# A two-stage feed-forward and attention kernel: the value product from split squares, one block later

## The reference

```python
x = x + 0.5 * ffn(layernorm(x), W_r, W_k, W_v, mu_r, mu_k)
x = x + attn(layernorm(x), Wk, bk, Wv, bv, ln_g, ln_b, Wo, bo)   # attn adds its own input too
x = x + 0.5 * ffn(layernorm(x), W_r, W_k, W_v, mu_r, mu_k)

# ffn: x_prev is x shifted by one token
xr = mu_r * x + (1.0 - mu_r) * x_prev
xk = mu_k * x + (1.0 - mu_k) * x_prev
out = sigmoid(xr @ W_r) * (square(relu(xk @ W_k)) @ W_v)
```

## Time and profile before

| engine | busy | share of the span |
|---|---|---|
| TensorE (PE) | 656.5 | 87% |
| TensorE weight loads (PEld) | 542.1 | 72% |
| VectorE (DVE) | 611.3 | 81% |
| ScalarE (ACT) | 418.0 | 56% |
| GpSimd (POOL) | 569.6 | 76% |

### The profile page before, as it was taken

How to read it: one execution, slowest core, us unless ns; L and a number is a source line. 1 busy time by engine, 2 the same in 40 slices (tenths; PEclk the granted TensorE clock), 3 DMA queues, 4 the chain that set the end, 5 groups by cost and what they waited for, 6 DMA issues and landing times. The chain is left out here.

```text
span 751.9 us, 13029 instructions
## 1 busy us (share of the span) xinstructions
PE 656.5 (87%) x3536; PEld 542.1 (72%) x3536; DVE 611.3 (81%) x1378; ACT 418.0 (56%) x743; POOL 569.6 (76%) x879
## 2 busy tenths in 40 slices
PE   2888988999779989988988998898867988988897
PEld 2777878888656667766766676676646878878786
DVE  5868667755679999999999999999976668667744
ACT  4666666664534544554455455445446676666652
POOL 3777778776378888888888888888853877788764
PEclk9999999999988999999999999999979999999999
DMA  7710000000000000000000000000000011011102
GB/s 246 231 57 0 0 0 0 0 1 1 0 0 1 1 0 0 0 0 0 0 0 0 0 0 0 0 0 1 1 1 0 29 57 56 30 54 56 56 29 85
DMA packets 18442, 18.67 MB, mean 25 GB/s; under 512 B 752, under 2 KB 18160, under 8 KB 18416
## 3 DMA queue, kind: packets, MB, share of 16 engines
q1 hardware_dynamic: 18416, 18.36, 7.5%
HBM read 9.97 MB, written 8.39 MB: 24 GB/s over the span
## 5 line engine op out<-in xcount | busy, mean ns | idle before, releaser
L222 POOL TENSOR_TENSOR bhalf<-xn 128x128 f32<-128x128 f32 x256 | 118.3, 493 | 30.4 <-DVE xn L567 30.4
L1135 PE MATMUL bank<-wkv,m_xnT 128*128 128x256 f32 x512 | 135.5, 395 | 5.3 <-DVE khat L561 3.3
L409 DVE TENSOR_TENSOR gating_buffers<-bank,gating_buffers 128x1024 f32<-128x1024 f32 x31 | 38.0, 1225 | 95.8 <-issue 55.0
L1079 PE MATMUL bank<-wffn,kact 128*128 128x256 f32 x512 | 115.8, 379 | 0.0
L1135 PEld LDWEIGHTS bank<-wkv,m_xnT 128*128 128x128 f32 x512 | 92.5, 196 | 25.1 <-issue 4.6
L953 POOL TENSOR_TENSOR res<-res,gating_buffers 128x1024 f32 (+1 forms) x31 | 75.2, 2426 | 39.1 <-DVE gating_buffers L409 39.1
L1079 PEld LDWEIGHTS bank<-wffn,kact 128*128 128x128 f32 x512 | 94.8, 190 | 11.6
L284 POOL TENSOR_TENSOR xk_lo<-xk,xk_hi 128x1024 fp32r<-128x1024 f32 x30 | 71.2, 2372 | 33.4 <-ACT xk_hi L712 33.4
L946 POOL TENSOR_TENSOR xr_lo<-xr,xr_hi 128x1024 fp32r<-128x1024 f32 x32 | 76.0, 2374 | 19.0 <-ACT xr_hi L718 16.8
L567 DVE TENSOR_TENSOR xn<-bank,khat 128x1024 f32<-128x1024 f32 x64 | 77.8, 1216 | 1.4
L567 DVE TENSOR_TENSOR gating_buffers<-bank,khat 128x1024 f32<-128x1024 f32 x64 | 77.6, 1212 | 0.0
(11 more groups left out here) (108 smaller groups left out, 1691.7 us busy)
## 6 DMA issues: line engine op xcount, KB each, us to landing
res<-x SPq DMA_DIRECT2D x16, 512.0 KB, 4.5
out<-res SPq DMA_DIRECT2D x15, 512.0 KB, 2.9
wkv<-w_kv SPq DMA_DIRECT2D x1, 512.0 KB, 8.0
out<-res SPq DMA_DIRECT2D x2, 256.0 KB, 2.1
wffn<-w_k SPq DMA_DIRECT2D x1, 256.0 KB, 3.8
wffn<-w_r SPq DMA_DIRECT2D x1, 256.0 KB, 4.6
wffn<-w_v SPq DMA_DIRECT2D x1, 256.0 KB, 6.0
wo<-w_o SPq DMA_DIRECT2D x1, 256.0 KB, 7.2
```

The costliest lines, as they stand in the source:

```text
L222: last = engine.tensor_tensor(o, a, b, op)
L1079: last = nc.tensor.matmul(dst[:, i, :], x[:, f, i * P:(i + 1) * P], wffn[:, w, f, :], start=f == 0, stop=f == FC - 1)
L1135: nc.tensor.matmul(dst[:, i, :], m_xnT[:, f, i * P:(i + 1) * P], wkv[:, f, col:col + D], start=f == 0, stop=False)
```

## The change

The square of the key product is written back to PSUM, over `k_ps`. It is then split as `xk` and `xr` are: ScalarE rounds it to `kact_hi` (`square_high`), VectorE subtracts this into `kact_lo` (`square_low`), both in fp32r and with two buffers, one for each b. The value product runs in three fp32r passes from these, for block s-1 behind key product s on TensorE. The weights of the value product are split too. On VectorE the receptance mixes come ahead of the squares, and gating of block s-1 behind them, followed by the low parts. GpSimd's program is unchanged. `bound` of the middle stage, which lay in `kact`, has its own buffer. Cut to its core:

```diff
-        wffn_hi = sb("wffn_hi", [P, 2, FC, D], F32R)
-        wffn_lo = sb("wffn_lo", [P, 2, FC, D], F32R)
+        wffn_hi = sb("wffn_hi", [P, 3, FC, D], F32R)
+        wffn_lo = sb("wffn_lo", [P, 3, FC, D], F32R)
...
-        kact = sb("kact", [P, FC, CW])
+        kact_hi = sb("kact_hi", [P, 2, FC, CW], F32R)
+        kact_lo = sb("kact_lo", [P, 2, FC, CW], F32R)
...
-        bound = kact[:, :, :].rearrange("p b (t n) -> p b t n", n=D)
+        bound = sb("bound", [P, 2, 2, D])
...
                     dve.wait_ge(e["relu_done"], 2 * s + o + 1)
-                    need(dve, e["v_done"], 2 * s)
-                    nc.vector.tensor_tensor(kact[:, o, :], relu_k[:, o, :], k_ps[:, o, :], ALU.mult).then_inc(e["kact_done"], 1)
+                    nc.vector.tensor_tensor(k_ps[:, o, :], relu_k[:, o, :], k_ps[:, o, :], ALU.mult).then_inc(e["kact_done"], 1)
+
+                def square_low(j, b, o):
+                    s = 2 * j + b
+                    dve.wait_ge(e["kacthi_done"], 2 * s + o + 1)
+                    need(dve, e["v_done"], 2 * (s - 1))
+                    nc.vector.tensor_tensor(kact_lo[:, b, o, :], k_ps[:, o, :], kact_hi[:, b, o, :].bitcast(F32),
+                                            ALU.subtract).then_inc(e["kactlo_done"], 1)
...
-                        if has(b, -1):
-                            gating(*at(j, b, -1))
                         if mixing:
                             difference(nj, nb)
                             mix_key(nj, nb, 0)
                             mix_key(nj, nb, 1)
+                            mix_receptance(nj, nb, 0)
+                            mix_receptance(nj, nb, 1)
                         if first:
                             stats_of(1, 1)
                         square(j, b, 0)
                         square(j, b, 1)
-                        if mixing:
-                            mix_receptance(nj, nb, 0)
-                            mix_receptance(nj, nb, 1)
+                        if has(b, -1):
+                            gating(*at(j, b, -1))
+                        square_low(j, b, 0)
+                        square_low(j, b, 1)
...
-            split_weights_low(1, 2)
+            split_weights_low(1, 3)
...
+                def square_high(j, b, o):
+                    s = 2 * j + b
+                    act.wait_ge(e["kact_done"], 2 * s + o + 1)
+                    need(act, e["v_done"], 2 * (s - 1))
+                    nc.scalar.copy(kact_hi[:, b, o, :], k_ps[:, o, :]).then_inc(e["kacthi_done"], 1)
...
                             receptance_high(*at(j, b, 1))
+                        square_high(j, b, 0)
+                        square_high(j, b, 1)
                         sigmoid(j, b)
...
                     pe.wait_ge(e["xklo_done"], s + 1)
-                    need(pe, e["kact_done"], 2 * s)
+                    need(pe, e["kactlo_done"], 2 * s)
...
-                    pe.wait_ge(e["kact_done"], 2 * s + 2)
+                    pe.wait_ge(e["kactlo_done"], 2 * s + 2)
                     need(pe, e["gated_done"], s)
-                    by_token(v_tok, kact, 2, 0, CT // 2).then_inc(e["v_done"], 1)
-                    by_token(v_tok, kact, 2, CT // 2, CT).then_inc(e["v_done"], 1)
+                    high, low = kact_hi[:, b, :, :], kact_lo[:, b, :, :]
+                    by_token(v_tok, high, low, 2, 0, CT // 2).then_inc(e["v_done"], 1)
+                    by_token(v_tok, high, low, 2, CT // 2, CT).then_inc(e["v_done"], 1)
...
                         key(j, b)
...
+                        if has(b, -1):
+                            value(*at(j, b, -1))
                         receptance(j, b)
                         if has(b, 2):
                             transposes(j + 1, b)
...
-                        value(j, b)
 
                 def steps():
                     rounds(pe, NJ, 1, 2, body)
+                    value(NJ - 1, 1)
```

More of the change, by code:

```diff
@@ L191, in macaron @@
                     "diff_done", "xk_done", "xkhi_done", "xklo_done", "xr_done", "xrhi_done", "xrlo_done", "k_done",
-                    "relu_done", "kact_done", "r_done", "gate_done", "v_done", "gated_done", "res_done"]
+                    "relu_done", "kact_done", "kacthi_done", "kactlo_done", "r_done", "gate_done", "v_done", "gated_done", "res_done"]
         ffn_sems = [{n: sem(f"f{i}_{n}") for n in FFN_SEMS} for i in range(2)]
@@ L336, in split_weights_high @@
                 nc.vector.tensor_scalar(cols_less_one[:, :], cols[:, 0:2 * FC], -1.0, None, ALU.add)
-                nc.vector.tensor_scalar(wffn[:, 2, :, :], wffn[:, 2, :, :], 0.5, None, ALU.mult)
-                own(nc.vector.tensor_copy(wffn_hi[:, :, :, :], wffn[:, 0:2, :, :]))
+                own(nc.vector.tensor_scalar(wffn[:, 2, :, :], wffn[:, 2, :, :], 0.5, None, ALU.mult))
+                own(nc.vector.tensor_copy(wffn_hi[:, :, :, :], wffn[:, :, :, :]))
             def split_weights_low(first, end):
@@ L1073, in key, with by_token @@
                               lambda f: xk_hi[:, f, :], lambda f: xk_lo[:, f, :]).then_inc(e["k_done"], 1)
-                def by_token(dst, x, w, first=0, end=CT):
+                def by_token(dst, x_hi, x_lo, w, first=0, end=CT):
                     for i in range(first, end):
-                        for f in range(FC):
-                            last = nc.tensor.matmul(dst[:, i, :], x[:, f, i * P:(i + 1) * P], wffn[:, w, f, :],
-                                                    start=f == 0, stop=f == FC - 1)
+                        last = parts(dst[:, i, :],
+                                     lambda f: x_hi[:, f, i * P:(i + 1) * P], lambda f: x_lo[:, f, i * P:(i + 1) * P],
+                                     lambda f: wffn_hi[:, w, f, :], lambda f: wffn_lo[:, w, f, :])
                     return last
@@ L1086, in receptance @@
                     need(pe, e["gate_done"], s)
[L1087 to L1091, removed]
+                    by_token(r_tok, xr_hi, xr_lo, 1).then_inc(e["r_done"], 1)
                 def value(j, b):
                     s = 2 * j + b
-                    pe.wait_ge(e["kact_done"], 2 * s + 2)
+                    pe.wait_ge(e["kactlo_done"], 2 * s + 2)
                     need(pe, e["gated_done"], s)
-                    by_token(v_tok, kact, 2, 0, CT // 2).then_inc(e["v_done"], 1)
-                    by_token(v_tok, kact, 2, CT // 2, CT).then_inc(e["v_done"], 1)
+                    high, low = kact_hi[:, b, :, :], kact_lo[:, b, :, :]
+                    by_token(v_tok, high, low, 2, 0, CT // 2).then_inc(e["v_done"], 1)
+                    by_token(v_tok, high, low, 2, CT // 2, CT).then_inc(e["v_done"], 1)
                 def body(j, has):
@@ L1106, in body @@
                             pe.wait_ge(weights_ready, 2)
+                            pe.wait_ge(bias_rows_ready, 2)
                         if stage == 1 and first:
                             pe.wait_ge(m["x_done"], MS)
+                        if has(b, -1):
+                            value(*at(j, b, -1))
                         receptance(j, b)
@@ L1111, in body @@
                             transposes(j + 1, b)
-                        if stage == 0 and first:
-                            pe.wait_ge(bias_rows_ready, 2)
-                        value(j, b)
                 def steps():
                     rounds(pe, NJ, 1, 2, body)
+                    value(NJ - 1, 1)
                 return transposes, steps
@@ L1190, in mem @@
                 pe.wait_ge(mem_ready, 1)
-                pe.wait_ge(ffn_sems[0]["kact_done"], FC * NS)
+                pe.wait_ge(ffn_sems[0]["kactlo_done"], FC * NS)
                 for b in range(2):
```

## The result

The changed kernel takes 837.58 (median of 4 runs, 836.34 to 838.13) against 754.78 of the kernel before: a ratio of 1.109, 95% interval 1.107 to 1.111, slower. The forecast was 842 with a range of 795 to 860. The profiled execution took 837.95, its span 835.9, and TensorE's mean granted clock 0.922 instead of 0.983.

The account below looks back on a forecast made before the run. Bound before: the loop value product, gating to `xr`, transposes, at 11.04 a block. The new loop of 12.33 with edges adds 43.4 to 753.64, giving 797; clock falls add 45, giving 842; range 795 to 860.

Parts of the forecast that it names:

- The loop: Key product, value product, gating, `residual`, `xk_lo`, next key product: period 12.33 against 11.04, 1.29 more per feed-forward block.
- nine measured pieces: Durations and hand-overs from one key product's start to the next, read from the earlier profile, summing to 12.33.
- VectorE's second chain up to gating: From the `xr_hi` cast through VectorE's mixes and squares, reaching gating about 6.0 after the next key product's start; taken as 0.
- The costs put at nothing: VectorE's squares written to PSUM, bounds 0 and another 0.6 per square, taken as 0.
- the bound of another 0.6 each: Upper bound on the extra time of each VectorE square written to PSUM; 0 was taken.
- The chain behind `xr_hi`: ScalarE's cast after the receptance, then casts of squares near 10.7, low parts near 11.5, wanted at 12.33.
- The clock: TensorE's 2.8 pause per block drops its clock in 6 of 10 blocks at 2.5: 1.5 a block, 45; chance 0.76.
- The rival in which the clock holds: TensorE's clock falls in no or few blocks despite the pauses: 797, range 795 to 815; chance 0.17.
- The edges: Stage ends: block 0 loses its value product, one is gained behind the last receptance; +2.2 per stage.
- The faster rival: `xk_lo` isn't held up by `residual` on GpSimd, block falls to TensorE's 9.36: 47 saved, 707; chance 0.02.

Follow-up runs that it names:

- experiment 2: Changed kernel plus 20 filler matmuls (result never read) behind each block's transposes, in TensorE's pause: 801.8, ratio 1.063.
- experiment 1: Changed kernel with GpSimd doing `residual` of block s-1 behind `xk_lo` and `xr_lo` of block s+1 instead of ahead: 811.5, ratio 1.076.
- experiment 4: Kernel before with only the move: plain fp32 value product one block later behind the key product, VectorE's order as in the change: 848.3, ratio 1.124.
- experiment 5: Changed kernel with the value product back in its own block, VectorE's old order, casts of squares ahead of the `xr_hi` cast: 749.4, ratio 0.993.
- experiment 3: Changed kernel plus 10 filler matmuls (result never read) behind each block's transposes, in TensorE's pause: 809.65, ratio 1.073.
- both queue positions: Changed kernel with `residual` behind `xr_lo` on GpSimd and the casts of the squares ahead of the `xr_hi` cast on ScalarE: 726.97, ratio 0.962.

## Why the prediction held

**The loop.** It was put at 12.33 from nine measured pieces; the trace after shows 12.16 in a block less its slow spell, and 12.3 on average with the clock held. The path is right; that 12.3 is met to the tenth is in part luck. The pieces come to nearly 0.2 less than forecast, and what the prediction put at nothing, VectorE's second chain up to gating, adds 0.2 in the mean once the clock holds (gating starts 6.06 behind K in experiment 2, and 5.86 where it doesn't wait for that chain). The key product takes 2.86 instead of 2.95, `residual` and `xk_lo` took 2.38 and 2.36 instead of 2.43 and 2.37, `xk_lo` starts 0.05 before `residual` is over and not 0.05 behind it, and the last hand-over is 0.14 instead of 0.05. Experiment 1 shows that `residual`'s place closes the loop, experiment 4 that the move puts it there, experiment 5 that the split doesn't.

**The costs put at nothing.** The squares written to PSUM take 1.29 for the pair against 1.28 before, and the low parts 1.29 too; the bound of another 0.6 each wasn't needed. The chain behind `xr_hi` was said to have the low parts ready at 11.5; with the first loop open a block without a slow spell took 11.6 (experiment 1), and they were what the key product waited for.

**The clock.** The total was right by luck: two of its factors were wrong and cancelled. A fall was expected in 6 of 10 blocks at 2.5 each, 1.5 a block, taking spells of 6.9 as in the earlier trace rows. It came in every steady block, in spells of 3.4 that cost 1.6. Held by filler, the clock gave back 36; the forecast had 45 for it. About 5 of the difference is the second chain (0.2 in each of 26 blocks), which shows only when the clock is whole. The rival in which the clock holds (797) is the kernel of experiment 2, 5 above its figure.

The Trainium skill, page "TensorE: Matmul & The Clock Gate", section "HAM oscillation — how this bites in real kernels", would have let these pauses pass. The traces disagree. In steady blocks, 2.5 to 2.8 brought a fall each time in the changed kernel and in 17 of 26 blocks of experiment 4, 2.1 to 2.2 in about two blocks of three (experiment 1), 1.4 to 2.0 in four of 26 (experiment 3), 0.99 never. And a single 3.42 brought none at the end of experiment 2. So the length of one pause does not decide it, and what else does stays open. The section behind it ("A second HAM failure mode: psum-queue depth-cycling"), on short idling between groups of matmuls, is nearer to what this kernel does.

**The edges.** 2.2 a stage were expected, 4.4 in all. The spans differ by 84.0, the two runs of key products by 38.86 + 38.68 = 77.5, so 6.5 is left: 2.6 between the stages (225.07 to 614.95 against 186.17 to 573.43) and 3.8 behind the last key product (17.2 against 13.4), of which a slow spell over that product is about 1.6. The forecast had 39.0 + 45 = 84.0 for the two runs of key products, 6.5 too much, and 2.1 too little for the edges.

**The faster rival** had its price wrong. It said that the block is TensorE's 9.36 and the time near 707 if gating's end didn't hold `xk_lo` up. With that hold gone and nothing else (experiment 1) the block was 11.6 and the time 811: the low parts behind `xr_hi`, which the prediction itself had at 11.5, set the block, and the rival's price left them out. With both queue positions mended the kernel ran at 9.75 and 727, so 27 of the 47 were saved.

## What to carry to other kernels

When a product is moved one block later, follow what its consumers stand ahead of in every queue: here the last of them, an addition that nobody was in a hurry for, stood ahead of the operand of the next block's first product, on an engine whose program the change did not touch. Look for the second wait behind the first before judging a mend; each of the two edits looked like 0 or 26, and both together were 111. And try the move of a few calls in the old kernel first: it had 33 to gain by order alone, as much as the best of the split versions.

## What the hardware showed

A pause of TensorE that recurs each block costs more than its own length. In the changed kernel a pause of 2.5 to 2.8 brought 3.4 at 1.2 GHz each time, worth 1.6 more, and 20 matmuls a block whose result nobody reads made the kernel faster by 36 of 838. The length of the pause alone doesn't tell a fall: with the same pauses experiment 4 had one in 17 of 26 blocks, and one pause of 3.42 in experiment 2 had none. The half-clock spells of steady blocks were 3.4 long in the changed kernel, while the one of the earlier trace rows was 6.9.
